# One attention chunk on TensorE: the small work that stood in the middle of four pairs of score matmuls goes behind them

## The reference

```
x = x + xcond(layernorm(x), ctx, ctx, k_length)   # cross attention over channels
x = x + moe(layernorm(x), Wg, w1, w2)             # 8 experts, top 2
```

## Time and profile before

| | |
|---|---|
| three runs | 2177.81, 2179.55, 2179.68 us, median 2179.55 |
| profiled execution | span 2177.8 us; the fastest of the runs is 2177.81, so nothing visible lies around the span |
| TensorE matmul busy | 2117.0 us, 97% of the span |
| VectorE, ScalarE, GpSimd busy | 1008.1, 712.9, 470.4 us |
| attention's loop of slots | begins at 24.30 us, ends at 615.31 us |
| experts | from 677 us to the end, 16 blocks of 512 rows, matmul behind matmul |

### The profile page before, as it was taken

How to read it: one execution, slowest core, us unless ns; L and a number is a source line. 1 busy time by engine, 2 the same in 40 slices (tenths; PEclk the granted TensorE clock), 3 DMA queues, 4 the chain that set the end, 5 groups by cost and what they waited for, 6 DMA issues and landing times. The chain is left out here.

```text
span 2177.8 us, 27085 instructions
## 1 busy us (share of the span) xinstructions
PE 2117.0 (97%) x10179; PEld 1518.8 (70%) x10179; DVE 1008.1 (46%) x1908; ACT 712.9 (33%) x1216; POOL 470.4 (22%) x593
## 2 busy tenths in 40 slices
PE   3999999999999999999999999999999999999997
PEld 1445454455547888878888887888888788888776
DVE  5677878878765434234324423423432342343211
ACT  1666666666652222113212212311311231132110
POOL 3334444343422111110301201031030102101101
PEclk9999999999999999999999999999999999999999
DMA  9876767776635435212613612422441252241101
GB/s 147 160 165 157 181 157 188 168 187 162 146 114 161 115 70 132 58 22 85 131 20 78 150 26 58 125 50 43 114 98 25 56 134 52 48 125 31 16 6 20
DMA packets 183895, 216.61 MB, mean 99 GB/s; under 512 B 39731, under 2 KB 111419, under 8 KB 183740
## 3 DMA queue, kind: packets, MB, share of 16 engines
q1 hardware_dynamic: 154128, 173.21, 34.1%
q0 software_dynamic: 22240, 37.92, 9.1%
q10 hardware_dynamic: 7372, 3.42, 0.7%
HBM read 113.93 MB, written 68.29 MB: 84 GB/s over the span
## 5 line engine op out<-in xcount | busy, mean ns | idle before, releaser
L1590 DVE SCALAR_TENSOR_TENSOR hlo<-ps_h,hhi 128x512 fp32r<-128x512 f32 x256 | 177.0, 692 | 928.4 <-ACT hhi L1467 928.4
L1467 ACT ACTIVATE hhi<-ps_h 128x512 fp32r<-128x512 f32 x256 | 152.9, 597 | 1123.4 <-PE ps_h L1731 1123.4
L1729 PE MATMUL ps_h<-xhi,w1hi 128*128 128x512 f32 x1024 | 404.9, 395 | 2.5 <-PEq L1316 1.3
L1748 PE MATMUL ps_y<-w2hi,hhi 128*128 128x512 f32 x1024 | 404.7, 395 | 0.7 <-DVE hlo L1590 0.7
L1749 PE MATMUL ps_y<-w2lo,hhi 128*128 128x512 f32 x1024 | 403.0, 394 | 1.0 <-issue 1.0
L1750 PE MATMUL ps_y<-w2hi,hlo 128*128 128x512 f32 x1024 | 403.7, 394 | 0.0
L1731 PE MATMUL ps_h<-xhi,w1lo 128*128 128x512 f32 x1024 | 403.6, 394 | 0.0
L1730 PE MATMUL ps_h<-xlo,w1hi 128*128 128x512 f32 x1024 | 403.0, 394 | 0.0
L678 DVE TENSOR_REDUCE nmax<-ps_s 128x1 f32<-128x512 f32 x512 | 335.7, 681 | 128.5 <-PE ps_s L1086 124.6
L460 ACT ACTIVATE probs<-ps_t 128x512 f32<-128x512 f32 x504 | 273.0, 604 | 183.1 <-PE ps_t L1037 145.8
L1729 PEld LDWEIGHTS ps_h<-xhi,w1hi 128*128 128x128 f32 x1024 | 192.3, 188 | 48.5 <-issue 3.9
(11 more groups left out here) (202 smaller groups left out, 2007.2 us busy)
## 6 DMA issues: line engine op xcount, KB each, us to landing
raw<-in_L_ffn_w SPq DMA_DIRECT2D x128, 512.0 KB, 4.9
qst<-qhi SPq DMA_DIRECT2D x64, 256.0 KB, 5.8
xin<-dispatched SPq DMA_DIRECT2D x60, 256.0 KB, 5.8
kst<-khi SPq DMA_DIRECT2D x52, 256.0 KB, 6.4
xt<-in_x SPq DMA_DIRECT2D x32, 256.0 KB, 3.1
ct<-in_ctx SPq DMA_DIRECT2D x32, 256.0 KB, 4.5
qst<-qlo SPq DMA_DIRECT2D x32, 256.0 KB, 6.8
xres<-in_x SPq DMA_DIRECT2D x32, 256.0 KB, 4.7
```

The costliest lines, as they stand in the source:

```text
L1467: nc.scalar.activation(hhi[k % 2][:], ps_h[k % 3][:], ACT.Relu).then_inc(hhi_ready, 1)
L1590: nc.vector.scalar_tensor_tensor(hlo[k % 2][:], ps_h[k % 3][:], 0.0, hhi[k % 2][:].bitcast(F32), ALU.max, ALU.subtract).then_inc(h_ready, 1)
L1729: nc.tensor.matmul(to, w1hi[:, c, fs], xhi[n % 2][:, c, :], start=(c == 0), stop=False)
L1748: nc.tensor.matmul(ps_y[b][:], hhi[k % 2][:, bs], w2hi[:, f, :], start=(f == 0), stop=False)
```

## The change

In TensorE's loop the three insertions lose their condition `i == 1` and move out of the loop over i, behind the pair i = 3 and ahead of the weighted sums. The numbering follows, so R, X, V and `lp` take other banks. ScalarE copies X and V after the chunk's four exponentials. VectorE's part for R moves from after the maximum (1,1) to after (1,3), that for `lp` from after (3,1) to after (3,3); there it stands behind the signal that the group's maxima are complete. No instruction is added or removed.

```diff
@@ bank_turns
-                if i == 1 and c == 2 and live(s - 5):
-                    t_turn["x2t", s - 5] = len(t_turn) + 1
-                if i == 1 and c == 2 and live(s - 1):
-                    t_turn["vt", s - 1] = len(t_turn) + 1
-                if i == 1 and c == 3 and (live(s - 5) or pair_in(s)):
-                    s_turn["lp", s] = len(s_turn) + 1
-                if i == 1 and c == 1 and live(s - 4):
-                    s_turn["r", s - 4] = len(s_turn) + 1
+            if c == 2 and live(s - 5):
+                t_turn["x2t", s - 5] = len(t_turn) + 1
+            if c == 2 and live(s - 1):
+                t_turn["vt", s - 1] = len(t_turn) + 1
+            if c == 3 and (live(s - 5) or pair_in(s)):
+                s_turn["lp", s] = len(s_turn) + 1
+            if c == 1 and live(s - 4):
+                s_turn["r", s - 4] = len(s_turn) + 1
@@ scalar
                         if live(s - 2):
                             powers(s - 2, c, i)
-                        if i == 1 and c == 2 and live(s - 5):
...
-                        if i == 1 and c == 2 and live(s - 1):
-                            values(s - 1)
...
+                    if c == 2 and live(s - 5):
...
+                        nc.scalar.activation(x2t[:], t_at(k)[:], ACT.Copy).then_inc(t_free, 1)
+                    if c == 2 and live(s - 1):
+                        values(s - 1)
@@ vector
-                        if (c, i) == (3, 1) and live(s - 5):
+                        if (c, i) == (1, 3) and live(s - 4):
+                            g = s - 4
+                            k = s_turn["r", g]
+                            dve.wait_ge(s_done, k)
+                            dve.wait_ge(o_saved, g + 1)
+                            nc.vector.tensor_tensor(o_sb[g % 2][:], s_at(k)[:], o_sb[g % 2][:], ALU.mult
+                                                    ).then_inc(s_free, 1)
+                        if (c, i) == (3, 3) and live(s):
+                            dve.wait_ge(s_free, s_turn["s", s, 3, 3])
+                            dve.sem_inc(nmax_done, 1)
+                        if (c, i) == (3, 3) and live(s - 5):
...
-                        if (c, i) == (3, 1) and pair_in(s):
+                        if (c, i) == (3, 3) and pair_in(s):
@@ tensor
                         if live(s - 2):
                             turned_logits(s - 2, c, i)
-                        if i == 1 and c == 2 and live(s - 5):
-                            row_turned(s - 5)
-                        if i == 1 and c == 2 and live(s - 1):
-                            values(s - 1)
-                        if i == 1 and c == 3 and (live(s - 5) or pair_in(s)):
...
-                        if i == 1 and c == 1 and live(s - 4):
-                            shares(s - 4)
+                    if c == 2 and live(s - 5):
+                        row_turned(s - 5)
+                    if c == 2 and live(s - 1):
+                        values(s - 1)
+                    if c == 3 and (live(s - 5) or pair_in(s)):
...
+                    if c == 1 and live(s - 4):
+                        shares(s - 4)
                     if c == 0 and live(s - 3):
                         weighted(s - 3, NC4 - 1)
```

More of the change, by code:

```diff
@@ L531, in _ @@
                                                      ).then_inc(rt["lexp"], 1)
+                    if c == 2 and live(s - 5):
+                        g = s - 5
+                        k = t_turn["x2t", g]
+                        act.wait_ge(t_done, k)
+                        if g >= 1:
+                            act.wait_ge(s_done, s_turn["lp", s - 1])
+                        nc.scalar.activation(x2t[:], t_at(k)[:], ACT.Copy).then_inc(t_free, 1)
+                    if c == 2 and live(s - 1):
+                        values(s - 1)
                     if c == 0 and live(s - 3):
@@ L783, in _ @@
                                                            ).then_inc(rt["place"], 1)
-                        if (c, i) == (3, 1) and (live(s - 5) or pair_in(s)):
+                        if (c, i) == (3, 3) and (live(s - 5) or pair_in(s)):
                             if live(s - 5):
@@ L789, in _ @@
                             dve.sem_inc(s_free, 1)
[L790 to L799, removed]
             def reciprocal(g):
@@ L1112, in _ @@
-                        if i == 1 and c == 1 and live(s - 4):
-                            shares(s - 4)
+                    if c == 2 and live(s - 5):
[3 more added lines that the diff above has]
+                    if c == 3 and (live(s - 5) or pair_in(s)):
+                        bank = s_bank(s_turn["lp", s])
+                        if pair_in(s):
+                            n = (s - 7) // 2 + 1
+                            pe.wait_ge(rt["before"], n)
+                            pos = bank[:, 2 * E:4 * E]
+                            nc.tensor.matmul(pos, earlier[:], picked[:].rearrange("p h e -> p (h e)"),
+                                             start=True, stop=False)
+                            done = nc.tensor.matmul(pos, ones[:], before[(n - 1) % 2][:].rearrange("p h e -> p (h e)"),
+                                                    start=False, stop=True)
+                        if live(s - 5):
+                            pe.wait_ge(t_free, t_turn["x2t", s - 5])
+                            if s == 5:
+                                pe.wait_ge(wg_ld, 16)
+                            for q in range(NC4):
+                                done = nc.tensor.matmul(bank[:, 0:E], x2t[:, P * q:P * q + P], wg_sb[:, q, :],
+                                                        start=(q == 0), stop=(q == NC4 - 1))
+                        done.then_inc(s_done, 1)
```

## The result

The changed kernel takes 2209.99 us (median of 4 runs, 2199.74 to 2221.71), the one before 2179.32 (4 runs beside them): a ratio of 1.0139, 95% interval 1.0104 to 1.0173. It is slower, by 30.7 us where 16 were forecast, and the time lies outside the range of 2184 to 2203. The profiled execution took 2205.21, with a span of 2203.5 against 2177.8.

What follows compares the result with a forecast made beforehand. TensorE, 97% busy, was taken to set the pace. Chunks 1, 2 and 3 gave 9.7 - 3.2 + 10.7 = +17.2, less some 0.3, so +17 and 2195.5 us; the range 2184 to 2203 held 8 in 10.

Steps and rivals of the forecast that it cites:

- the two waits and their price: Chunk 1's last T waits for ScalarE's first exponential, +9.7 us; chunk 3's insertion for VectorE's second maximum, +10.7.
- the 0.10 of a stall beside its wait: On TensorE, a held-up matmul's weights aren't loaded in advance, costing 0.10 us on top of its wait.
- the 5.31 that slot 3 gave: Chunk 1's higher estimate: slot 3's chunk without R takes 4.89 us, plus 0.42 for R before W.
- rival 4: On TensorE a stall costs its wait only, without the 0.10: +11.5 us, 2190; chance 20%.
- no clock level is at stake: TensorE's granted clock was 1.00, the level of 2.4 GHz, throughout the slots' 550.27 us; no clock loss forecast.
- Rival 3: Slots cascade: delayed ScalarE copies or VectorE hold later work, 0.49 us more a slot; +30, 2209; chance 7%.
- the price of V before W: Chunk 2: V directly before W adds +0.05 us, making X and V 0.90 instead of 0.85.
- to save 3.2: Chunk 2 takes 4.74 us against 4.86, one switch saved: -0.12, 27 times.
- the 1.2 for DMA-late R: Chunk 1: ten R waited for their DMA, 5.7 us in all; issuing R later takes about 1.2 from +10.9.

Runs made afterwards that it cites:

- e5: Changed kernel with ScalarE issuing the denominators' DMA (l_wide) after chunk 1's first exponential instead of before it; 2188.56 us, ratio 1.0030 to the kernel before.
- e4: Changed kernel with VectorE's row statistics and their sum after maxima (3,2) and (3,3) instead of (3,0) and (3,1); 2190.56 us, ratio 1.0017 to the kernel before.
- e6: Changed kernel with both the e4 and e5 edits; 2166.89 us, ratio 0.9924 to the kernel before.
- e3: Kernel before with only chunk 3's insertion (P and G, lp) moved behind the four pairs; 2204.23 us, ratio 1.0068.
- e9: e6 with X and V of chunk 2 back behind the second pair; 2169.17 us, ratio 0.9931 to the kernel before.
- e2: Kernel before with only chunk 2's insertion (X and V) moved behind the four pairs; 2192.57 us, ratio 1.0027.
- e1: Kernel before with only chunk 1's insertion (R) moved behind the four pairs; 2197.6 us, ratio 1.0048.
- e10: Kernel before with the e4 and e5 edits and nothing moved; 2181.39 us, ratio 0.9984.
- before_again: The kernel before itself, run once more without any edit; 2181.18 us, one run.
- e8: Kernel before with only the e5 edit; 2180.81 us, ratio 0.9983.

## Why the prediction was wrong

The direction (slower, at 89%) was right, and most of the sum too; the size was not.

*Right: the two waits and their price.* Chunk 1 was forecast at 5.28 and takes 5.29; chunk 3 at 5.31 and 5.76 and takes 5.31 and 5.76. e5 takes away what chunk 1 waits for and its T starts at 1.76; e4 takes away what `lp` waits for and chunk 3 falls below the kernel before.

*Right: the 0.10 of a stall beside its wait.* R follows a held T after 0.43 here, and chunk 1 stays under the 5.31 that slot 3 gave. For `lp` the runs show the term by itself: P to W takes 1.44 behind the wait and 1.34 without it (e4, e6), G to W 0.98 and 0.89. So rival 4 falls. The prediction read the Trainium skill, "TensorE: Matmul & The Clock Gate", Part 3 (The mechanism), as leaving no head start to lose, and the trace disagrees with the sentence that it took. The same section of the Trainium skill also says that a load can be pulled ahead into a background weight buffer, and with that sentence the trace agrees (the load at 76.38 inside the matmul of 76.27 to 76.77).

*Wrong: "no clock level is at stake".* This is the step that failed. The prediction read the clock of the kernel before and carried it over, so the loss by the clock was put at nothing. In the changed kernel P starts 0.73 behind T (324.57 to 325.30), where it was due after 0.24, and 1.44 us of matmuls of 16 and 8 columns follow before W, in a pair slot's chunk 3. In 3 of 13 such chunks of one profile and in 12 of 13 of another the clock falls to its lower level a few tenths into W, for 3.4 us, and about 1.6 is lost. Of the 30.7 us this is the part over the 22.2 of the slots, 8.5 at the median.

How firm is that? In the four profiles with this wait (the changed kernel twice, e3, e5) the clock fell in 23 of 52 such chunks. In three with P and G in the same place and no wait (e4, e6, e9) it fell in none of 39; in the other seven P stands between T and S, and it fell in none of 91. In the 28 slots without P of the changed kernel's two profiles, where the same wait is followed by 1.0 us of narrow matmuls, it never came. Since falls come in series, chunks of one profile aren't independent trials; but the mean clocks of all the runs point the same way: the 27 with the wait reach down to 0.987, the 21 of e4, e6 and e9 only to 0.993 (e5, which has the wait, doesn't go lower than that either). The falls are what makes 2201.5 into 2210 or 2220, and they are no term of any rival; which executions get many of them isn't known. Rival 3 names a sum near the measured one (2209) for another reason, and its mechanism isn't there, since the plain chunks stay 3.93.

*Wrong: the price of V before W.* V to W was bounded by 0.38 and 0.42 + 0.09 = 0.51 and taken as 0.43; it is 0.56, above the upper bound. X also starts 0.26 behind T and V 0.49 behind X, against 0.24 and 0.47. Chunk 2 was to save 3.2 and loses 1. e2 shows it alone, and e9 undoes it. This is the largest error in the sum itself. The upper bound was built from R before W, a matmul of 8 rows, so it bounded nothing for V's four matmuls of 128x128; a price that no row shows needs a wider range than two neighbours give.

*Right in size: the 1.2 for DMA-late R.* The two chunks that were read have a mean of 4.885, all 28 one of 4.93, since a few of them are longer (5.01 to 5.36, two of these with a late R): 28 times 0.04 is 1.2. In the changed kernel no R waits for its DMA, ScalarE's wait has taken that place, and all 28 take 5.29.

The sum then: 10.1 + 1.1 + 4.5 + 6.5 = 22.2 in place of 17, and 1.64 for each fall of the clock, three and twelve of them in the two profiles. Without the falls the time would be about 2201.5, inside the range.

## What to carry to other kernels

Before a small piece of work is moved behind a run, ask which buffer the run itself will wait for. Here gathering work on the busiest engine paid only once the releasers (the DMA issue with its wait on ScalarE, the statistics on VectorE) had been moved out of the way, and the repairs were worth more with the move than alone.

A short wait in a dense stream, followed by narrow matmuls, cost more than itself here through TensorE's clock. A forecast that adds such a wait in every round should carry "the clock falls each time" as a rival with its own price.

A time that spreads by 1% between runs, with the mean clock going along, calls for a second profile before the first one is explained. And a total that agrees with a term is no proof of it: in e1 the chunks had to be counted one by one.

## What the runs showed of the hardware

- **The clock falls in a busy engine.** TensorE ran at 1.2 GHz for 3.4 us without stopping, after 0.34 us idle and 1.4 us of matmuls of 16 and 8 columns. The same matmuls without the wait (39 times in e4, e6 and e9) did not bring it, nor did chunk 1's wait of 0.67 before one R (28 times in each of the changed kernel's profiles). Longer waits of R for its DMA did, with the insertion in its old place: 1.10 in e2, 1.24 in e10, 1.50 in before_again, 1.81 in e3; but another of 1.5 in e10 (R at 563.72) did not. And five profiles (e1, e2, e3, e4, e8) have one fall in a last chunk 3 with G, between 593 and 619 us, after the standstill of the last point. "TensorE: Matmul & The Clock Gate" of the Trainium skill says (Terms) that the penalty is the time at the lower level times the part of the clock that is missing: 3.4 x 0.5 = 1.7, and the trace agrees with 1.64.
- **It repeats with the kernel's period.** In the second profile every fall is 41 us behind the last, in every pair slot but the first. In the first profile it is two in a row (473.77 and 514.72) and one at the end; in e3 it is first every second pair slot, 78.5 us apart (197.77 to 433.70). In two runs of six there is, by their clock and time, hardly any. The same program on the same chip gives 2201.8 or 2221. What decides it is shown by no run here. "TensorE: Matmul & The Clock Gate" of the Trainium skill (Part 1, What's actually happening) calls the hardware's look at activity free-running: it doesn't start anew with the kernel. By that rule two groups of runs would be no surprise, but nothing here tests it.
- **What stands before W matters.** R costs 0.42 before W and 0.43 before S (188.37 to 188.80), but X and V together 1.05 before W (333.50 to 334.55) and 0.85 before S.
- **Two engines stood still together** for some 2.2 us: eight times in e2 with no releaser on this core for VectorE, six times for ScalarE too. In the last chunk 3 with G of five profiles (e1, e2, e3, e4, e8) both again start within 0.04 us of each other, 1.4 to 2.5 into the chunk (e1: 606.86 and 606.90), though the profile names TensorE there. The cause is open.
